# A Macaron block on one core: new order of the head, and weight preparation moved between engines and steps

## Chip, cores and metric

The kernel runs on one core of a Trainium2 chip. The metric is the time of one execution in microseconds, the median of the runs made. In the profile PE is TensorE (PEld its weight loads), DVE is VectorE, ACT is ScalarE, POOL is GpSimd, SP is SyncE, which only issues DMAs here.

## The reference

`x` has the shape (4, 512, 512). The block adds half of a routed FFN, then causal attention with 32 query heads in 8 groups (head size 128, rotary positions), then half of the same FFN again:

```python
x = x + 0.5 * ffn(layernorm(x))
x = x + attn(layernorm(x))
x = x + 0.5 * ffn(layernorm(x))
...
def ffn(h):
    query = h @ Wq.T
    router_scores = (query @ Wr.T) @ (aux_keys @ Wr.T).T / sqrt(48) + log_rel
    top_idx = top_k(router_scores, 8)
    w = softmax(query . aux_keys[top_idx] / sqrt(64) + log_rel[top_idx])
    aux_out = (w @ aux_values[top_idx]) @ Wvd.T @ Wvu.T
    log_var = log1p(var(h))
    learned = gelu(h @ Wu1.T + bu1) @ Wu2.T + bu2
    u = clip(log_var / (mean(log_var) + 1e-6) * 0.5 + sigmoid(learned) * 2.5, 0, 5)
    gate = sigmoid(gate_w1 * clip((u - 0.5) / 1.5, 0, 1) + gate_bias)
    return h + where(gate < 0.05, 0, gate) * aux_out
```

The mean of `log_var` runs over all 2048 rows, so the gate of the first row needs the variances of the whole input.

## The kernel before

**Tiles.** X stays in SBUF as 16 tiles of 128 rows. Every fp32 operand of a large matmul is split into a high part (bf16 or fp16, a cast on ACT) and a low part (the rest in fp16, a subtraction on POOL or DVE), and a product is three matmuls (`mm3`, L1522 to L1524). Attention's weights come as 256 KB pieces (K, Q0 to Q3, V and W0 to W3 for each of 8 groups). A piece is loaded into one of 8 slots of `raw` (`raw_load`, L486), its high part is a cast on ACT (`weight_high`, L801), its low part a subtraction on POOL (`weight_low`, L621) or, for the pieces in `BYDVE`, on DVE (L1201). Pieces 0 to 3 get both parts on POOL. Then the piece is kept in HBM (`keep`, L510), and batches 1 to 3 load it from there (`load_kept`, L519). `raw_load(r)` needs the low part of piece r-8, and SP issues all of this in one order.

**The head** (0 to about 69 us) is written out by hand for each engine. It does the first FFN for batch 0 and prepares the first 16 pieces. SP and ACT issue the loads. `bu2`, `gw`, `gb` (three loads of 0.5 KB, L505) are the last that count on the semaphore `ld_fs`; DVE waits for all six of that semaphore before its first `take_scores` (L1080). Then, for each of four tiles, DVE takes the scores out of PSUM and picks the top eight (`top`, L1095 to L1104), which lets ACT take the exponentials (`exps_ffn`, L781) and PE transpose them ("ET", L1592). Row sums and sums of squares of tiles 6 to 10 (`sums`, L852) are ACT's, the statistics of the others DVE's (L1022). After all variances are there (`moments_of_sums`, L1261 to L1264, `variance_logs`, L1123 to L1125) ACT takes the logarithms (`logs`, L775), DVE sums them (L1129), PE adds over the partitions ("MEAN", L1586), and the gates follow (`gs`, L1169). `aux_first` (L1271) adds the FFN to X, the second layer norm is normalised (L1059) and transposed (L1542), and the projections of group 0 begin. PE's tasks take PSUM banks in turn in the order of the list `HEAD`: a task waits until the one four places earlier is consumed. GELU needs a table load on ACT before it and another behind it (L764, L771).

**The loop** has 128 steps, one for each batch, group and head. In a step DVE takes the masked minima of the scores (`minima`, L1237), makes the low part of the step before's probabilities (`p_lo`, L1247), the reciprocal of the sums (L1389) and three products for the rotation of a later query (L1191 to L1193). POOL adds them (L629) and makes the query's low part (L634), ACT the exponentials (L831) and high parts. SP transposes the probabilities by DMA (`turn`, L526), two issues a step, behind that step's loads and keeps. In batch 0 the steps also prepare pieces 16 and on: `REFILL` says which pieces belong to which of a group's four steps; `MADE_AT` is the step in which a piece is made. It is kept two steps later, and the load of the piece eight places later follows the keep. FFN work of the next batch (`side`) is spread over the steps by tables. In step 0 DVE refines the deviation of tiles 4 to 15 (`deviation`, L1036 to L1040, `base_factors`, L1044, L1045); steps 0 and 1 normalise the first two tiles of batch 1 (L1059).

Of the kernel before, what the change touches and what calls it, by code (L numbers as in the profile page):

```python
# [12 lines left out]
P = 128  # L13
# [16 lines left out]
NSPLIT = 4  # L30
BYDVE = range(6, 11)

# [24 lines left out]
NRAW = 8  # L57
# [48 lines left out]
def rest_of(n, h):  # L106
# [4 lines left out]

HEAD = ([("LT", 0, 0, i) for i in range(4)] + [("QRY", 0, 0, 0), ("SCR", 0, 0, 0), ("SCR", 0, 0, 1), ("HID", 0, 0, 0), ("ET", 0, 0, 0),
        ("HOUT", 0, 0, 0), ("MEAN", 0, 0, 0)] + [("AUX", 0, 0, i) for i in range(4)] + [("LT", 1, 0, i) for i in range(4)])
FIRST = [("V", 0, 0, 0), ("K", 0, 0, 0), ("Q", 0, 0, 0), ("Q", 0, 1, 0)]
# [34 lines left out]
def prepared(engine, what):  # L149
    return PREPARED[engine].index(what) + 1  # L150

REFILL = {0: [(1, "Q1"), (1, "V"), (-1, "W3")], 1: [(1, "Q2")], 2: [(1, "Q3"), (2, "K"), (0, "W0")],
          3: [(2, "Q0"), (0, "W1"), (0, "W2")]}
# [23 lines left out]
for s_ in range(NS):  # L179
    for it_ in made(s_):  # L180
        ITEMS.append(it_)
        MADE_AT.append(s_)
ITEM = {it: r for r, it in enumerate(ITEMS)}
NHEAD = len(HEAD_ITEMS)


def macaron_kernel(nc: bass.Bass, x, wqkv, wo, bo, cosq, sinq, cosk, sink,
# [3 lines left out]
    with ctx:  # L191
# [289 lines left out]
        def _(sp):  # L481
# [20 lines left out]
            load_x(12, 4)  # L502
            for dst, src in ((bu2[:, :], f_bu2.to_broadcast([P, 1])), (gw[:, :], f_gw.to_broadcast([P, 1])),
                             (gb[:, :], f_gb.to_broadcast([P, 1]))):
                sp.dma_start(dst, src).then_inc(ld_fs, 16)  # L505

# [48 lines left out]
            for s in range(NS):  # L555
                for n, kind in refills(s):
                    if n >= G or (n, kind) in STAGED:
                        load_kept(n, kind)
                for r in range(NHEAD, len(ITEMS)):
                    if MADE_AT[r] + 2 == s:  # L560
                        keep(r)
                for r in range(NHEAD + NRAW, len(ITEMS)):
                    if MADE_AT[r - NRAW] + 2 == s:
                        raw_load(r)
                if s:
                    turn(s - 1, 0)
                    turn(s - 1, 1)
                for _, k, bb, i in side(SP_A, SP_B, s):
                    turn_normal(k, bb, i)
# [9 lines left out]
        def _(pool):  # L579
# [76 lines left out]
            nc.gpsimd.tensor_tensor(ul[:, :, :], fwu1T, uh[:, :, :], ALU.subtract).then_inc(fu_lo, 1)  # L656
            pool.wait_ge(x_ab[0], 1)
            for n in range(4):
                nc.gpsimd.tensor_scalar(X[:, n, :], X[:, n, :], xa[:, 0, n:n + 1], xb[:, 0, n:n + 1], ALU.mult,
                                        ALU.add).then_inc(x_up[0], 1)  # L660
            for r in range(NSPLIT):
                weight_low(r)
            pool.wait_ge(r_gs[0], 1)
            for r in range(NSPLIT, BYDVE[0]):
                weight_low(r)
            pool.wait_ge(rope_lo, 2)
            pool.wait_ge(w_lo, BYDVE[-1] + 1)
            weight_low(BYDVE[-1] + 1)
            rope("Q", 0, 1)
            for r in range(BYDVE[-1] + 2, NHEAD):  # L670
                weight_low(r)
# [31 lines left out]
        def _(act):  # L703
            roots, totals = [0], [0]
            for n in (0, 2):
                act.dma_start(X[:, n:n + 2, :], x_v[:, n:n + 2, :]).then_inc(ld_x[n], 16)
            for dst, src in ((lrb[:, :], f_lr.to_broadcast([P, NSLOT])), (bu1[:, :], f_bu1), (wu2T[:, :], f_wu2T)):
                act.dma_start(dst, src).then_inc(ld_fs, 16)
# [146 lines left out]
            def sums(n):  # L855
                act.wait_ge(ld_x[n // 4 * 4], 16)
                total(n, ACT.Identity, s1[:, 0, n:n + 1])
                total(n, ACT.Square, s2[:, 0, n:n + 1])
# [22 lines left out]
            nc.scalar.activation(bh[:, 0:NSLOT], SC[:, 1, 0:NSLOT], ACT.Copy, scale=fqs[:, 0:1]).then_inc(fs_act, 1)  # L881
            nc.scalar.activation(bh[:, NSLOT:2 * NSLOT], fkeyT[:, :], ACT.Copy, scale=fqs[:, 0:1]).then_inc(fs_act, 1)
            query_hi(0, 0, 0)
            query_hi(0, 0, 1)
            act.wait_ge(ld_fu, 16)
            nc.scalar.copy(uh[:, :, :], fwu1T).then_inc(fs_act, 1)
            for n in BYACT[:3]:
                sums(n)
            exps_ffn(0, 0, (0, 1))
            sums(BYACT[3])  # L890
            exps_ffn(0, 0, (2, 3))
            sums(BYACT[4])
            act.wait_ge(ld_fs, 96)
            gelu(0, 0)
            e_hi(0, 0)
            gate_exp(0, 0, 4)
            logs(0)
            act.wait_ge(fs_pe, prepared("pe", "v2"))
            nc.scalar.copy(v2h[:, :], PV[:, :]).then_inc(fs_act, 1)
            weight_high(4)  # L900
            gate_exp(1, 0, 4)
# [111 lines left out]
        def _(dve):  # L1013
# [305 lines left out]
            query_lo(0, 0, 1)  # L1319
            base_factors(0, 0, 4)  # L1320
            arrived(4)
            arrived(5)
            dve.wait_ge(ld_fs, 96)
            for i in range(2):
                take_scores(0, 0, (i,))
                top(0, 0, (i,))
            dve.wait_ge(ld_x[8], 16)
            moments(0, 11)
            arrived(12)
            for i in range(2, 4):  # L1330
                take_scores(0, 0, (i,))
                top(0, 0, (i,))
            for n in range(13, NT):
                moments(0, n)
            dve.wait_ge(fs_pe, prepared("pe", "u1T"))
            nc.vector.tensor_copy(u1T[:, :], SC[0:VB, 0, 0:NSLOT]).then_inc(fs_dve, 1)
            variance(0, 4, NT)
            moments_of_sums()
            dve.wait_ge(ln_v[0], 3)
            variance_logs(0)  # L1340
            learned(0, 0)
            gate_1(0, 0, 4, 1)
            e_lo(0, 0)
            sigmoid(0, slice(0, 4))
            log_sum(0)
            dve.wait_ge(fs_act, prepared("act", "v2"))
            nc.vector.tensor_tensor(v2l[:, :], PV[:, :], v2h[:, :], ALU.subtract).then_inc(fs_dve, 1)
            inverse_sums(0, 0, 4, 1)
            log_mean(0)
# [10 lines left out]
            for i in range(4):  # L1360
                turned_lo(1, 0, i)
            for r in BYDVE:
                weight_low(r)
# [11 lines left out]
            for s in range(NS):  # L1375
                n, h = divmod(s, HG)
                par = s % 2
                minima(s)
                if s == 0:
                    deviation(0, 1, 4, NT)  # L1380
                    base_factors(0, 4, NT)
                if s:
# [11 lines left out]
                for stage, k, bb, i in side(DVE_A, DVE_B, s):  # L1394
                    if stage == "nrm":
                        normal(k, bb, i)
# [121 lines left out]
        def _(pe):  # L1518
# [220 lines left out]
            ins.then_inc(fs_pe, 1)  # L1739
            ffn_task(("ET", 0, 0, 0))  # L1740
            pe.wait_ge(fs_dve, prepared("dve", "u1T"))
            mm(PV[:, :], u1T[:, :], fwvuT, start=True, stop=True).then_inc(fs_pe, 1)
            pe.wait_ge(ld_fs, 96)
            ffn_task(("HOUT", 0, 0, 0))
            ffn_task(("MEAN", 0, 0, 0))
# [84 lines left out]
```

## Time and profile before

| | us |
|---|---|
| median of three runs | 1433.54 (1432.22 to 1436.56) |
| the profiled execution | 1431.55 |
| its span | 1429.8 |
| PE busy | 1359.9 |
| DVE busy | 1184.8 |
| ACT busy | 954.0 |
| POOL busy | 701.2 |
| granted clock, mean | 0.985 |

The span is the time from the first to the last instruction; 1.75 us lie around it. Steps of the loop begin 10 to 11 us apart.

### The profile page before, as it was taken

What the parts mean: (1) busy time and instruction counts of PE and PEld (TensorE: products, weight loads), DVE (VectorE), ACT (ScalarE), POOL (GpSimd) and SP (SyncE); (2) the same over time, 40 slices, a digit from 0 to 9 for tenths busy, and PEclk for the clock granted to TensorE, in tenths of its full rate; (3) what the DMA queues carried; (4) which work ended last, traced back from release to release, by engine and by line L of the source; (5) the groups of instructions that cost most, each with busy time, mean ns of one, the idle gap of its engine ahead of it and who ended that gap; (6) DMA issues with size and microseconds to landing.
All of it is one profiled execution on the core that took longest, in us unless ns stands there. A gap on an engine that the chain in (4) does not pass through costs nothing.

```text
span 1429.8 us, 25974 instructions
## 1 busy us (share of the span) xinstructions
PE 1359.9 (95%) x8604; PEld 751.9 (53%) x8604; DVE 1184.8 (83%) x2880; ACT 954.0 (67%) x2463; POOL 701.2 (49%) x593
## 2 busy tenths in 40 slices
PE   4778999998999999999999999999999999999996
PEld 2444555454555555555555555555555555555553
DVE  6897978899988898988878798889777798778657
ACT  4567786776677677666766676667666676666754
POOL 3176666767764444345545354444544454434321
PEclk8799999999999999999999999999999999999998
DMA  8356767779677566566658656656576666556443
GB/s 302 119 138 150 191 163 186 186 173 219 171 151 163 127 144 151 118 130 148 141 124 168 130 131 146 122 134 148 138 143 127 146 142 154 116 134 135 94 88 118
DMA packets 439829, 211.21 MB, mean 148 GB/s; under 512 B 382016, under 2 KB 383344, under 8 KB 439696
## 3 DMA queue, kind: packets, MB, share of 16 engines
q1 hardware_dynamic: 438576, 208.18, 63.3%
q8 instruction: 69, 1.13, 0.3%
q10 hardware_dynamic: 1120, 1.38, 0.3%
q14 instruction: 64, 0.52, 0.1%
HBM read 91.00 MB, written 25.17 MB: 81 GB/s over the span
## 4 chain that ended last, share of the span: by engine, by line
PE 77%; DVE 12%; ACT 3%; issue 3%; POOL 2%; DMA 1%; SPq 1%; DVEq 0%; ACTq 0%
PE PJ L1522 17%; PE PJ L1524 17%; PE PJ L1523 17%; PE PV L1695 4%; PE PV L1690 4%; PE PV L1691 4%; PE SC L1709 4%; PE SC L1711 4%; PE SC L1710 4%; DVE phl L1247 3%; DVE p L1237 2%; POOL t L629 2%; DVE t L1193 1%; DVE t L1192 1%; DVE t L1191 1%
## 5 line engine op out<-in xcount | busy, mean ns | idle before, releaser
L651 POOL TENSOR_TENSOR oTl<-of,oTf 128x512 f16<-128x512 f32 x128 | 154.1, 1204 | 439.3 <-ACT oTf L823 439.0
L831 ACT ACTIVATE p<-p,mn 128x512 f32<-128x512 f32 (+3 forms) x512 | 280.9, 549 | 95.4 <-DVE mn L1237 95.4
L1247 DVE SCALAR_TENSOR_TENSOR phl<-p,ri,phl 128x128 f16<-128x128 f32 (+3 forms) x512 | 331.5, 687 | 0.0
L842 ACT ACTIVATE phl<-p,ri 128x128 f16<-128x128 f32 (+3 forms) x512 | 245.6, 550 | 4.1
L1522 PE MATMUL PJ<-XT,wsp 128*128 128x512 f16 x628 | 238.9, 380 | 4.8 <-DVE t L1193 4.8
L629 POOL TENSOR_TENSOR t<-t 128x512 f32<-128x512 f32 x158 | 201.4, 1275 | 76.4 <-DVE t L1193 75.9
L1524 PE MATMUL PJ<-XT,wsp 128*128 128x512 f16 x628 | 238.8, 380 | 0.0
L1523 PE MATMUL PJ<-XT,wsp 128*128 128x512 f16 x628 | 238.7, 380 | 0.0
L1237 DVE CUSTOM_DVE_ANT_0 p<-SC,maskw 128x512 f32<-128x512 f32 (+3 forms) x512 | 219.8, 485 | 2.2
L1522 PE MATMUL PJ<-wosp,oTf 128*128 128x512 bf16 x512 | 194.1, 379 | 0.0
L1524 PE MATMUL PJ<-wosp,oTl 128*128 128x512 bf16 x512 | 194.1, 379 | 0.0
L1523 PE MATMUL PJ<-wosp,oTf 128*128 128x512 f16 x512 | 194.1, 379 | 0.0
L634 POOL TENSOR_TENSOR qTl<-t,qTh 128x512 f16<-128x512 f32 x127 | 148.3, 1167 | 92.5 <-ACT qTh L807 92.5
L807 ACT CAST qTh<-t 128x512 bf16<-128x512 f32 x128 | 79.1, 618 | 138.2 <-POOL t L629 136.1
L1690 PE MATMUL PV<-pTf,vh 128*128 128x512 f16 (+3 forms) x512 | 146.9, 301 | 12.4 <-DMA pTf<-phl 12.4
L1709 PE MATMUL SC<-kTh,qTh 128*128 128x512 bf16 (+3 forms) x512 | 147.3, 301 | 8.4 <-DVE mn L1237 5.7
L1710 PE MATMUL SC<-kTl,qTh 128*128 128x512 f16 (+3 forms) x512 | 153.9, 301 | 0.0
L1711 PE MATMUL SC<-kTh,qTl 128*128 128x512 bf16 (+3 forms) x512 | 147.3, 301 | 0.0
L822 ACT ACTIVATE of<-PV 128x512 f32<-128x512 f32 x128 | 75.2, 587 | 96.2 <-PE PV L1695 96.2
L1691 PE MATMUL PV<-pTf,vl 128*128 128x512 f16 (+3 forms) x512 | 133.1, 301 | 0.0
L1224 DVE TENSOR_TENSOR X<-PJ,X 128x512 f32<-128x512 f32 x124 | 85.0, 686 | 35.2 <-PE PJ L1524 34.0
L1524 PEld LDWEIGHTS PJ<-XT,wsp 128*128 128x128 f16 x628 | 61.5, 98 | 74.6 <-issue 0.8
(263 smaller groups left out, 2588.7 us busy)
## 6 DMA issues: line engine op xcount, KB each, us to landing
wsp<-kept SPq DMA_DIRECT2D x146, 256.0 KB, 3.0
wosp<-kept SPq DMA_DIRECT2D x96, 256.0 KB, 3.4
raw<-in_wqkv SPq DMA_DIRECT2D x48, 256.0 KB, 4.7
kept<-wsp SPq DMA_DIRECT2D x42, 256.0 KB, 2.4
raw<-in_wo SPq DMA_DIRECT2D x32, 256.0 KB, 4.7
kept<-wosp SPq DMA_DIRECT2D x32, 256.0 KB, 3.0
pTf<-phl SPq DMA_TRANSPOSE x256, 3.8
X<-in_x SPq DMA_DIRECT2D x3, 1024.0 KB, 9.6
```

The lines of the kernel that those rows point to most:

```text
L629: ins = nc.gpsimd.tensor_tensor(t1[:, j, c], t1[:, j, c], t2[:, j, c], ALU.add)
L831: ins = nc.scalar.activation(pt, pt, ACT.Exp, bias=mn[:, par, i:i + 1], scale=-1.0, accum_out=rs[:, par, i:i + 1])
L842: nc.scalar.activation(phl[:, par, high(i, 0):high(i, i) + 1:3, :], p[:, par, SOFF[i]:SOFF[i] + w].rearrange("p (k t) -> p k t", t=P), ACT ...
L1237: ins = nc.vector.tensor_tensor_reduce(out=p[:, par, SOFF[i]:SOFF[i] + w], in0=SCf[:, SOFF[i]:SOFF[i] + w], in1=maskw[:, T - w:T], scale=1 ...
L1247: nc.vector.scalar_tensor_tensor(out=phl[:, par, low(i, 0):low(i, i) + 1, :], in0=p[:, par, SOFF[i]:SOFF[i] + w].rearrange("p (k t) -> p k ...
L1522: mm(out_, lh, rh, start=start, stop=False)
L1523: mm(out_, lh, rl, start=False, stop=False)
L1524: return mm(out_, ll, rh, start=False, stop=stop)
L1690: mm(PV[:, j * P:T], vh[:, n % 2, j, :], hi, start=j == 0, stop=False)
L1709: mm(o, qh, kh, start=True, stop=False)
L1710: mm(o, qh, kl, start=False, stop=False)
L1711: ins = mm(o, ql, kh, start=False, stop=True)
```

## The change

- The three small loads `bu2`, `gw`, `gb` are issued by ACT behind its own, and no longer by SP.
- The head is reordered. DVE selects tiles 0 and 1 before it takes the statistics of tiles 4 and 5, takes `u1T` ahead of tiles 2 and 3, and has `learned` and `gate_1` before the last five statistics. ACT copies `uh` before the queries, takes GELU before any exponentials, and puts its sums between them. PE does HOUT before the product for `v2` and before ET.
- POOL waits for the first two selections before it scales X, and for all four before it makes the low parts of pieces 0 to 3. It now makes 6, 7 and 8 too, after the second layer norm's tiles are normalised, and 12 ahead of the rotation of Q1. DVE keeps 9 and 10 only.
- The deviation of tiles 4 to 15 and the normalisation of batch 1's first two tiles leave steps 0 and 1 and stand before DVE's low parts and the rotation of K.
- A group's V piece is loaded or made in step 1 of four, not in step 0. A raw load comes one step before its piece is made (for W2 in the same step), a keep two steps after (for W2 three).

```diff
-BYDVE = range(6, 11)
+BYDVE = range(9, 11)
...
-HEAD = ([...] + [("QRY", 0, 0, 0), ("SCR", 0, 0, 0), ("SCR", 0, 0, 1), ("HID", 0, 0, 0), ("ET", 0, 0, 0),
-        ("HOUT", 0, 0, 0), ("MEAN", 0, 0, 0)] + ...
+HEAD = ([...] + [("QRY", 0, 0, 0), ("SCR", 0, 0, 0), ("SCR", 0, 0, 1), ("HID", 0, 0, 0), ("HOUT", 0, 0, 0),
+        ("ET", 0, 0, 0), ("MEAN", 0, 0, 0)] + ...
...
-REFILL = {0: [(1, "Q1"), (1, "V"), (-1, "W3")], 1: [(1, "Q2")], 2: [(1, "Q3"), (2, "K"), (0, "W0")],
+REFILL = {0: [(1, "Q1"), (-1, "W3")], 1: [(1, "Q2"), (1, "V")], 2: [(1, "Q3"), (2, "K"), (0, "W0")],
           3: [(2, "Q0"), (0, "W1"), (0, "W2")]}
...
+RAW_AT = [at - (0 if kind == "W2" else 1) for at, (n, kind) in zip(MADE_AT, ITEMS)]
+KEEP_AT = [at + (3 if kind == "W2" else 2) for at, (n, kind) in zip(MADE_AT, ITEMS)]
...
-            for dst, src in ((bu2[:, :], f_bu2.to_broadcast([P, 1])), (gw[:, :], f_gw.to_broadcast([P, 1])),
-                             (gb[:, :], f_gb.to_broadcast([P, 1]))):
-                sp.dma_start(dst, src).then_inc(ld_fs, 16)
...
-                    if MADE_AT[r] + 2 == s:
+                    if KEEP_AT[r] == s:
                         keep(r)
...
-                    if MADE_AT[r - NRAW] + 2 == s:
+                    if RAW_AT[r] == s:
                         raw_load(r)
...
             pool.wait_ge(x_ab[0], 1)
+            pool.wait_ge(r_mn[0], 2)
             for n in range(4):
                 nc.gpsimd.tensor_scalar(X[:, n, :], ...).then_inc(x_up[0], 1)
+            pool.wait_ge(r_mn[0], 4)
             for r in range(NSPLIT):
                 weight_low(r)
             pool.wait_ge(r_gs[0], 1)
-            for r in range(NSPLIT, BYDVE[0]):
+            for r in range(NSPLIT, 6):
                 weight_low(r)
-            pool.wait_ge(rope_lo, 2)
+            pool.wait_ge(ln_h[1], 4)
+            for r in range(6, BYDVE[0]):
+                weight_low(r)
             pool.wait_ge(w_lo, BYDVE[-1] + 1)
             weight_low(BYDVE[-1] + 1)
+            pool.wait_ge(rope_lo, 2)
+            weight_low(BYDVE[-1] + 2)
             rope("Q", 0, 1)
-            for r in range(BYDVE[-1] + 2, NHEAD):
+            for r in range(BYDVE[-1] + 3, NHEAD):
                 weight_low(r)
...
+            act.wait_ge(ld_fu, 16)
+            nc.scalar.copy(uh[:, :, :], fwu1T).then_inc(fs_act, 1)
             query_hi(0, 0, 0)
             query_hi(0, 0, 1)
-            act.wait_ge(ld_fu, 16)
-            nc.scalar.copy(uh[:, :, :], fwu1T).then_inc(fs_act, 1)
-            for n in BYACT[:3]:
-                sums(n)
-            exps_ffn(0, 0, (0, 1))
-            sums(BYACT[3])
-            exps_ffn(0, 0, (2, 3))
-            sums(BYACT[4])
+            sums(BYACT[0])
+            sums(BYACT[1])
             act.wait_ge(ld_fs, 96)
             gelu(0, 0)
-            e_hi(0, 0)
-            gate_exp(0, 0, 4)
-            logs(0)
+            exps_ffn(0, 0, (0, 1))
             act.wait_ge(fs_pe, prepared("pe", "v2"))
             nc.scalar.copy(v2h[:, :], PV[:, :]).then_inc(fs_act, 1)
+            sums(BYACT[2])
+            exps_ffn(0, 0, (2, 3))
+            gate_exp(0, 0, 4)
+            sums(BYACT[3])
+            e_hi(0, 0)
+            sums(BYACT[4])
+            logs(0)
...
             base_factors(0, 0, 4)
+            dve.wait_ge(ld_fs, 96)
+            select_first(0)
+            select_first(1)
             arrived(4)
             arrived(5)
-            dve.wait_ge(ld_fs, 96)
-            for i in range(2):
-                take_scores(0, 0, (i,))
-                top(0, 0, (i,))
+            dve.wait_ge(fs_pe, prepared("pe", "u1T"))
+            nc.vector.tensor_copy(u1T[:, :], SC[0:VB, 0, 0:NSLOT]).then_inc(fs_dve, 1)
+            select_first(2)
+            select_first(3)
+            learned(0, 0)
+            gate_1(0, 0, 4, 1)
             dve.wait_ge(ld_x[8], 16)
             moments(0, 11)
             arrived(12)
-            for i in range(2, 4):
-                take_scores(0, 0, (i,))
-                top(0, 0, (i,))
             for n in range(13, NT):
                 moments(0, n)
...
             variance_logs(0)
-            learned(0, 0)
-            gate_1(0, 0, 4, 1)
+            sigmoid(0, slice(0, 4))
             e_lo(0, 0)
-            sigmoid(0, slice(0, 4))
-            log_sum(0)
             dve.wait_ge(fs_act, prepared("act", "v2"))
             nc.vector.tensor_tensor(v2l[:, :], PV[:, :], v2h[:, :], ALU.subtract).then_inc(fs_dve, 1)
+            log_sum(0)
...
                 turned_lo(1, 0, i)
+            deviation(0, 1, 4, NT)
+            base_factors(0, 4, NT)
+            normal(0, 1, 0)
+            normal(0, 1, 1)
             for r in BYDVE:
                 weight_low(r)
...
-                if s == 0:
-                    deviation(0, 1, 4, NT)
-                    base_factors(0, 4, NT)
...
-            ffn_task(("ET", 0, 0, 0))
+            pe.wait_ge(ld_fs, 96)
+            ffn_task(("HOUT", 0, 0, 0))
             pe.wait_ge(fs_dve, prepared("dve", "u1T"))
             mm(PV[:, :], u1T[:, :], fwvuT, start=True, stop=True).then_inc(fs_pe, 1)
-            pe.wait_ge(ld_fs, 96)
-            ffn_task(("HOUT", 0, 0, 0))
+            ffn_task(("ET", 0, 0, 0))
```

`select_first(i)` is `take_scores` and `top` of tile i.

## Rows read from the trace of the kernel before

**Rows 1.** One stretch: length; busy PE, PEld, DVE, ACT, POOL (instructions); clock; DMA share; GB/s.

```profile
84.00:108.00 24.00, 16.38 (x128) 9.42 (x126) 22.00 (x40) 15.32 (x39) 16.06 (x13) 1.00 0.58 110
```

**Rows 2.** What TensorE waited for, 130 to 370 us: total, times, longest.

```profile
PE PV L1690 <- DMA pTf<-phl: 6.7, 3, 4.0
...
PE PJ L1522 <- DVE t L1193: 4.8, 3, 2.4
```

**Rows 3.** The same view, 370 to 1370 us.

```profile
PE PV L1695 <- DMA pTf<-phl: 0.4, 1, 0.4
```

**Rows 4.** Chain that ended last: start, length, what.

```profile
14.96 8.82 DMA gb<-in_f_gb
```

**Rows 5.** Timeline of VectorE, head: start, length, line, operation, count, idle before.

```profile
18.68 1.28 DVE L1022 BATCH_NORM_STATS2 st<-X 128x6 f32<-128x512 f32 x2
...
23.81 0.29 DVE L1080 SCALAR_TENSOR_TENSOR rsc<-PJ,lrb 128x128 f32<-128x128 f32 x1 [3.85 <-DMA gb<-in_f_gb]
...
28.98 1.28 DVE L1022 BATCH_NORM_STATS2 st<-X 128x6 f32<-128x512 f32 x2
...
30.18 0.27 DVE L1080 SCALAR_TENSOR_TENSOR rsc<-PJ,lrb 128x128 f32<-128x128 f32 x1
...
33.59 1.87 DVE L1022 BATCH_NORM_STATS2 st<-X 128x6 f32<-128x512 f32 x3
...
36.05 0.15 DVE L1261 TENSOR_SCALAR s<-s 128x5 f32<-128x5 f32 x1
...
37.20 0.17 DVE L1125 TENSOR_TENSOR gv<-mv,nv 128x16 f32<-128x16 f32 x1
...
41.36 0.17 DVE L1129 TENSOR_REDUCE lsum<-lv 128x1 f32<-128x16 f32 x1
```

**Rows 6.** DMA issues of the first 70 us: queue, count, KB, us to landing.

```profile
wu2T<-in_f_wu2T ACTq DMA_DIRECT2D x1, 0.5 KB, 7.5
```

**Rows 7.** Timeline of GpSimd, head.

```profile
19.90 3.02 POOL L659 TENSOR_SCALAR X<-X,xa,xb 128x512 f32<-128x512 f32 x4
...
22.86 0.62 POOL L616 CAST wsp<-raw 128x512 bf16<-128x512 f32 x1
...
28.99 1.15 POOL L621 TENSOR_TENSOR wsp<-raw,wsp 128x512 f16<-128x512 f32 x1
```

**Rows 8.** Timeline of ScalarE, head.

```profile
18.51 0.72 ACT L852 ACTIVATE t<-X 128x512 f32<-128x512 f32 x1
...
22.65 0.19 ACT L852 ACTIVATION_READ_ACCUMULATOR t<-X 128x1 f32 x1
...
38.01 1.28 ACT L771 ACT_TABLE_LOAD   x1
```

**Rows 9.** VectorE's small operation in step 0, and GpSimd beside it.

```profile
71.21 1.17 DVE L1039 TENSOR_SCALAR nw<-nw 128x12 f32<-128x12 f32 x1
...
72.31 2.27 POOL L621 TENSOR_TENSOR oTl<-raw,oTl 128x512 f16<-128x512 f32 x2
```

**Rows 10.** Timeline of TensorE, head.

```profile
41.68 0.55 PE L1586 MATMUL PJ<-lsum,ones 128*128 128x1 f32 x2 [1.71 <-DVE lsum L1129]
```

**Rows 11.** VectorE between the second layer norm's transposes and the rotation of K.

```profile
56.16 2.49 DVE L1201 TENSOR_TENSOR wosp<-raw,wosp 128x512 f16<-128x512 f32 x4
...
59.60 0.69 DVE L1191 TENSOR_TENSOR t<-PJ,ck 128x512 f32<-128x512 f32 x1 [0.36 <-PE PJ L1524]
```

**Rows 12.** VectorE and GpSimd in steps 0 to 2.

```profile
76.79 1.59 DVE L1059 TENSOR_SCALAR hb<-X,mv,rstd 128x512 f32<-128x512 f32 x1
...
76.84 1.26 POOL L629 TENSOR_TENSOR t<-t 128x512 f32<-128x512 f32 x1
...
94.36 0.18 DVE L1389 RECIPROCAL ri<-rs 128x4 f32<-128x4 f32 x1 [1.80 <-ACT p L831]
```

**Rows 13.** SyncE's queue in a step of the second batch.

```profile
714.21 0.32 SPq L519 DMA_DIRECT2D wosp<-kept  x1
...
717.44 3.97 SPq L526 DMA_TRANSPOSE pTf<-phl  x2
```

More of the change, by code:

```diff
@@ L109, in rest_of @@
     return [t for t in r if 0 <= t[1] < NU]
-HEAD = ([("LT", 0, 0, i) for i in range(4)] + [("QRY", 0, 0, 0), ("SCR", 0, 0, 0), ("SCR", 0, 0, 1), ("HID", 0, 0, 0), ("ET", 0, 0, 0),
-        ("HOUT", 0, 0, 0), ("MEAN", 0, 0, 0)] + [("AUX", 0, 0, i) for i in range(4)] + [("LT", 1, 0, i) for i in range(4)])
+HEAD = ([("LT", 0, 0, i) for i in range(4)] + [("QRY", 0, 0, 0), ("SCR", 0, 0, 0), ("SCR", 0, 0, 1), ("HID", 0, 0, 0), ("HOUT", 0, 0, 0),
+        ("ET", 0, 0, 0), ("MEAN", 0, 0, 0)] + [("AUX", 0, 0, i) for i in range(4)] + [("LT", 1, 0, i) for i in range(4)])
 FIRST = [("V", 0, 0, 0), ("K", 0, 0, 0), ("Q", 0, 0, 0), ("Q", 0, 1, 0)]
@@ L706, in _ @@
                 act.dma_start(X[:, n:n + 2, :], x_v[:, n:n + 2, :]).then_inc(ld_x[n], 16)
-            for dst, src in ((lrb[:, :], f_lr.to_broadcast([P, NSLOT])), (bu1[:, :], f_bu1), (wu2T[:, :], f_wu2T)):
+            for dst, src in ((lrb[:, :], f_lr.to_broadcast([P, NSLOT])), (bu1[:, :], f_bu1), (wu2T[:, :], f_wu2T),
+                             (bu2[:, :], f_bu2.to_broadcast([P, 1])), (gw[:, :], f_gw.to_broadcast([P, 1])),
+                             (gb[:, :], f_gb.to_broadcast([P, 1]))):
                 act.dma_start(dst, src).then_inc(ld_fs, 16)
@@ L1320, in _, with select_first @@
             base_factors(0, 0, 4)
+            dve.wait_ge(ld_fs, 96)
+            def select_first(i):
+                take_scores(0, 0, (i,))
+                top(0, 0, (i,))
+            select_first(0)
+            select_first(1)
             arrived(4)
             arrived(5)
-            dve.wait_ge(ld_fs, 96)
-            for i in range(2):
-                take_scores(0, 0, (i,))
-                top(0, 0, (i,))
+            dve.wait_ge(fs_pe, prepared("pe", "u1T"))
[4 more added lines that the diff above has]
+            gate_1(0, 0, 4, 1)
             dve.wait_ge(ld_x[8], 16)
@@ L1329, in _ @@
             arrived(12)
-            for i in range(2, 4):
-                take_scores(0, 0, (i,))
-                top(0, 0, (i,))
             for n in range(13, NT):
                 moments(0, n)
-            dve.wait_ge(fs_pe, prepared("pe", "u1T"))
-            nc.vector.tensor_copy(u1T[:, :], SC[0:VB, 0, 0:NSLOT]).then_inc(fs_dve, 1)
             variance(0, 4, NT)
@@ L1394, in _ @@
                 for stage, k, bb, i in side(DVE_A, DVE_B, s):
-                    if stage == "nrm":
+                    if stage == "nrm" and (k, bb, i) not in ((0, 1, 0), (0, 1, 1)):
                         normal(k, bb, i)
```

## The prediction

> **What bounds the kernel now.** I read three views in this order: PE's waits by stretch, the chain that ended last, and the timelines of the head. From 370 to 1370 us PE waited for 0.4 us in all [rows 3]: there it is the bound, its work is unchanged, and nothing done to other engines can save time. Time can be won only where PE stands idle: in the head, in the first steps of the loop (PE busy 16.4 of 24 us against VectorE's 22.0, [rows 1]), and in single waits of batch 0 [rows 2]. What PE saves there moves the whole rest forward.
>
> In the head the chain lies for 8.82 us on the load of `gb` [rows 4]. SP issued it at 14.96 us behind a dozen others, and VectorE, done with two statistics at 19.9, stood idle for 3.85 us until 23.81 [rows 5]. From there VectorE's four selections, ScalarE's exponentials and sums, the variances, the logarithms and the mean follow in one chain up to MEAN at 41.68 [rows 10]. Behind MEAN the change leaves the order as it is up to the transposes of the second layer norm. So I work out when MEAN starts, then what changes behind it.
>
> **Part 1, the gates' loads.** They are now issues four to six of ScalarE's own group, some 0.45 us each, so out by about 4.6 us. The load in front of them took 7.5 us to land [rows 6]; the slowest of the three took 8.8 in its old place [rows 4]. They land by 13.5 us at the worst, 5 us before they are needed. ScalarE's table load slips by 1.4 us, covered by its wait for the first variances. So the selections start at about 18.7 instead of 23.8.
>
> **Part 2, up to the mean.** Two tiles without GpSimd beside them took 30.18 to 33.59, 1.7 us each; with it 23.81 to 28.98, 2.6 each [rows 5]. The new waits keep GpSimd away from tiles 0 and 1: done at 22.1. Two statistics (1.2 us at their pitch) and `u1T` (0.2) bring 23.6, two more tiles 27.0. GpSimd's four scalings of X, 3.02 us [rows 7], now lie beside tile 2; I add 0.5 (bounds 0 and 1.8, what four tiles' neighbours cost before): 27.6. `learned`, `gate_1`, five statistics at 0.6 and seven aggregates (0.5) end at 31.6 on VectorE. ScalarE's way is longer: each `sums` costs 1.42 us (three of them, six operations with their reads, lay from 18.51 to 22.84), a table load 1.28 [rows 8]. Two sums end at 21.0, the loads and GELU at 24.3, then two exponentials, v2 and one sums (27.5); exponentials 2 and 3 end at 28.6, and two sums, `e_hi` and a gate operation bring 32.3. The chain of variances then runs on VectorE: 36.05 to 37.37, 1.32 us for seven operations [rows 5]. Alone that gives 33.6.
>
> But GpSimd now begins pieces 0 to 3 behind the last selection, at about 27.9. They took 22.86 to 30.14, 7.3 us [rows 7], so it works until 35.2, on top of this chain. Before, it stood idle there. How such small operations fare is seen in step 0: 12 columns took 1.17 us where they take 0.17 alone, ending with GpSimd's operation in progress [rows 9]; the reciprocal beside it was not held. So until 35.2 one VectorE operation passes per GpSimd operation, about three of the seven, and four more cost 0.8: 36.0. The bounds are 33.6 (none held) and 36.0 plus 1.0 (each of the first four meets a long one). I take 36.0, nearest to those rows. By the seven operations' own rows, 0.15 to 0.25 us each, it would be 33.6 and the head 2.4 us shorter. The Trainium skill (GPSIMD Engine Reference, Key points) lists contention "with DVE instructions in a 2-port perf mode or with two SBUF inputs"; five or six of the seven are of these kinds, so by that rule they are held, and it speaks against the place chosen for pieces 0 to 3.
>
> Behind it come two operations of the sigmoid, `e_lo` and `v2l`, 1.6 us, now ahead of the sum of the logarithms: 37.6, MEAN at 37.9 in place of 41.68 [rows 10]. **Term: -3.8** (bounds -6.1 and -2.8).
>
> **Part 3, before the loop.** Of five low parts on VectorE, 2.49 us for four [rows 11], two stay (1.24). Added are four linked operations (0.8), the base factors (0.2) and two normalisations (0.5 each when alone): 3.3 in place of 3.1, and there were 0.36 us idle before the rotation of K [rows 11]. That alone is even. GpSimd, idle there before, now makes piece 8 beside the linked operations: one is held by about a microsecond. The rotation of K and the whole chain to the first scores on VectorE slip. **Term: +0.9** (bounds 0 and +3, every added operation held once).
>
> **Part 4, steps 0 to 2.** VectorE loses 3.7 us of the deviation and its factors (held to over 1 us each, [rows 9]) and two normalisations of 1.59 [rows 12]. Step 0's minima must wait for ScalarE's exponentials anyway, so of this 2.7 us reach step 1, and 1.6 more step 2. But the query's path runs over GpSimd, whose addition began at 76.84 right behind its low parts [rows 12]; one part fewer there lets it start 1.0 us earlier. In step 2 VectorE had to wait 1.80 us for exponentials [rows 12], which hang on that path. So what arrives at step 3 is about 2 us. **Term: -2.0** (bounds 0 and -4.3).
>
> **Part 5, pieces in batch 0.** Per four steps it was 3, 1, 3, 3 pieces with 6, 2, 6, 6 keeps and loads; now 2, 2, 3, 3 with five in each step. PE's waits that this can touch are 6.7 us for transposed probabilities, the longest 4.0 behind a step with seven transfers, and 4.8 us for rotations [rows 2]. The raw loads come later, but still a step ahead of the cast. The 4.0 should shrink by the two transfers fewer, the rest moves at random. **Term: -1.5** (bounds -5 and +2). In batches 1 to 3 V's load moves too; PE waits there for nothing [rows 3]: 0.
>
> **Sum:** -3.8 + 0.9 - 2.0 - 1.5 = -6.4. The profiled execution took 1431.55 us (span 1429.8 and 1.75 around it), which gives 1425.2. The median of the three runs lies 2.0 above it, so I forecast 1427.
>
> **Rivals.**
> *Not held (better).* The variance chain passes GpSimd, or the sums end earlier: -6.1; nothing held before the loop: 0; steps 0 to 2: -4; batch 0: -3. In all -13, 1420.5. For it: the bounds of each term. Against: [rows 9]. Chance 0.2.
> *The head gains, the loop gives nothing.* Steps 0 to 2 are set by GpSimd and ScalarE, not by VectorE, and batch 0's waits only change places: -3.8 + 0.9 = -2.9, 1430.6. For it: VectorE's 1.80 us of waiting in step 2 with ScalarE as its releaser. Against: VectorE's 22.0 of 24 us busy. Chance 0.22.
> *Slower: V's load before the probabilities.* In step 1 of each group SP issues two loads instead of one ahead of the transposes. If these are already late, each of the 24 groups of batches 1 to 3 loses the issue, about 0.5 us: +12, net +6, 1439. It decides from the point where less than 0.5 us lies between the loads and the transposes. Against: the last load of such a step was out at 714.5 and the transposes began at 717.44 [rows 13], and steps with three loads cost PE nothing [rows 3]. Chance 0.05.
> *The change does nothing.* Had `gb` not been the true last, selections would still start at 23.8. But X, scores and bias were there before 19.9. Chance 0.03.
>
> **Numbers.** The forecast case has 0.5, with a range of its own from 1423.5 to 1430. What a measurement here can tell from no change is 0.3%, 4.3 us: faster is below 1429.2. That takes in the better rival and most of the forecast's case, 0.72; within 0.3% the second rival, the fourth and the forecast's rest, 0.23; slower 0.05. The range 1418 to 1431.5 reaches into the two neighbouring rivals.
>
> **What the profile after should show.** No wait of VectorE for `gb`, selections from 18.7. MEAN at 37 to 38; if it is near 35.5, nothing was held. Operations of L1261 to L1125 with a microsecond each if I am right. K's rotation 52 to 57 us (before 59.60). The fourth step's scores some 5 us earlier than before. PE's waits between 130 and 370 us at 10 to 14 us. I am wrong if `sums` (L852) end well after 32.3, or if waits for `pTf` turn up after 420 us.

## The result and the profile after

| | median, us | runs | ratio to before | 95% interval |
|---|---|---|---|---|
| before | 1434.25 | 4 | | |
| after | 1426.04 | 4 | 0.9945 | 0.9926 to 0.9964 |

The change is faster by 0.55% (0.36% to 0.74%), about 8 us. The forecast was 1427 with 1418 to 1431.5. The profiled execution took 1426.41 us, its span 1423.6, 6.2 less than before. Measured again beside other kernels, the same kernel gave 0.9942 (0.993 to 0.9955).

Between the two traces the span fell by 6.2 us and the whole time by 5.1, while the medians fell by 8.2. The profiled execution of before (1431.55) was 2.7 us faster than its median, that of after 0.4 slower than its own. Only one trace of before exists, and no trace shows where its slower executions lose their time.

Where the 6.2 us of the traces came from can be read by lining them up at the same work (a shift is after minus before; a step begins with VectorE's first minima):

| where | before, us | after, us | shift |
|---|---|---|---|
| first selection starts | 23.81 | 18.93 | -4.88 |
| MEAN starts | 41.68 | 37.03 | -4.65 |
| second layer norm's transposes | 51.50 | 46.53 | -4.97 |
| rotation of K starts | 59.60 | 55.66 | -3.94 |
| step 0, VectorE's first minima | 69.16 | 65.22 | -3.94 |
| step 1 | 78.31 | 71.60 | -6.71 |
| step 2 | 89.58 | 82.38 | -7.20 |
| step 3 | 98.91 | 93.08 | -5.83 |
| step 34 | 428.22 | 422.77 | -5.45 |

The timeline of VectorE after (columns as in [rows 5]) shows the selections without a wait for `gb`, and then the variance chain, whose first and last operation before stand in [rows 5]:

```profile
18.93 0.28 DVE L1089 SCALAR_TENSOR_TENSOR rsc<-PJ,lrb 128x128 f32<-128x128 f32 x1
...
20.64 0.29 DVE L1089 SCALAR_TENSOR_TENSOR rsc<-SC,lrb 128x128 f32<-128x128 f32 x1
...
23.75 0.27 DVE L1089 SCALAR_TENSOR_TENSOR rsc<-PJ,lrb 128x128 f32<-128x128 f32 x1
...
25.98 0.29 DVE L1089 SCALAR_TENSOR_TENSOR rsc<-SC,lrb 128x128 f32<-128x128 f32 x1
...
32.12 0.17 DVE L1270 TENSOR_SCALAR s<-s 128x5 f32<-128x5 f32 x1
32.32 1.00 DVE L1271 TENSOR_TENSOR mv<-X,s 128x5 f32<-128x5 f32 x1
...
33.42 0.46 DVE L1273 SCALAR_TENSOR_TENSOR mv<-s,dm 128x5 f32<-128x5 f32 x1
...
34.13 0.25 DVE L1133 RECIPROCAL nv<-nv 128x16 f32<-128x16 f32 x1
34.42 0.72 DVE L1134 TENSOR_TENSOR gv<-mv,nv 128x16 f32<-128x16 f32 x1
...
36.72 0.16 DVE L1138 TENSOR_REDUCE lsum<-lv 128x1 f32<-128x16 f32 x1
```

Two operations of the same chain in before:

```profile
36.23 0.17 DVE L1262 TENSOR_TENSOR mv<-X,s 128x5 f32<-128x5 f32 x1
...
36.91 0.25 DVE L1124 RECIPROCAL nv<-nv 128x16 f32<-128x16 f32 x1
```

The second operation took 1.00 us where it took 0.17 before, the last 0.72, also for 0.17; the reciprocal between took 0.25 as before. GpSimd beside them (after, timeline; before it is [rows 7]):

```profile
22.64 3.01 POOL L660 TENSOR_SCALAR X<-X,xa,xb 128x512 f32<-128x512 f32 x4 [4.91 <-DVE mnr L1113]
27.84 0.61 POOL L616 CAST wsp<-raw 128x512 bf16<-128x512 f32 x1 [2.19 <-DVE mnr L1113]
...
32.11 1.18 POOL L621 TENSOR_TENSOR wsp<-raw,wsp 128x512 f16<-128x512 f32 x1
33.24 0.62 POOL L616 CAST wsp<-raw 128x512 bf16<-128x512 f32 x1
33.95 1.16 POOL L621 TENSOR_TENSOR wsp<-raw,wsp 128x512 f16<-128x512 f32 x1
...
51.39 1.16 POOL L621 TENSOR_TENSOR wosp<-raw,wosp 128x512 f16<-128x512 f32 x1 [1.28 <-ACT wosp L809]
```

VectorE's held operations ended at 33.32, 33.88 and 35.14; GpSimd's operations in progress ended at 33.29, 33.86 and 35.11. The last row is piece 8. It holds the first of the added operations on VectorE in front of the rotation of K (1.14 us). These are VectorE's rows in the place of [rows 11]:

```profile
51.43 1.14 DVE L1045 TENSOR_TENSOR nw<-rstd 128x12 f32<-128x12 f32 x1
52.61 0.17 DVE L1046 SCALAR_TENSOR_TENSOR nw<-mv,nw 128x12 f32<-128x12 f32 x1
...
53.39 1.00 DVE L1068 TENSOR_SCALAR hb<-X,mv,rstd 128x512 f32<-128x512 f32 x2
...
55.66 0.69 DVE L1200 TENSOR_TENSOR t<-PJ,ck 128x512 f32<-128x512 f32 x1
```

What PE waited for, 60 to 125 us, then 125 to 370 us ([rows 2] begin at 130), then 370 to 1370 us [rows 3], three views of after:

```profile
PE PV L1703 <- DMA pTf<-phl: 4.1, 2, 2.6
PE SC L1722 <- POOL qTl L634: 2.8, 2, 1.4
PE SC L1722 <- DVE mn L1246: 2.6, 1, 2.6
```

```profile
PE PJ L1535 <- DVE t L1202: 3.9, 3, 2.1
PE PV L1703 <- DMA pTf<-phl: 2.6, 1, 2.6
PE PV L1708 <- DMA pTf<-phl: 2.0, 1, 2.0
```

```profile
PE PV L1703 <- DMA pTf<-phl: 1.1, 1, 1.1
PE PV L1708 <- DMA pTf<-phl: 1.1, 2, 0.8
```

Each row gives the total, the number of times and the longest, in us. From 370 us on nearly all is at the end of batch 0 (at 372.75 and 374.83 us); behind that PE is all but free of waits, as before. Between steps 3 and 28 all of PE's listed waits came to 19.7 us before and 16.5 after. PE's busy time there rose from 252.3 to 255.1 us and the stretch took 0.4 us longer, so the shorter waits bought no time. What lengthened the busy time is not shown.

### The profile page after: what moved, and what is told of

Read it like the earlier page. It is cut to its first block, busy times and chain, and to the rows that moved or that the text cites. A ratio compares the mean times of both kernels' runs of the same rounds, so it can differ in the third digit from the quotient of the medians.

```text
span 1423.6 us, 25847 instructions
## 1 busy us (share of the span) xinstructions
PE 1351.8 (95%) x8474; PEld 754.3 (53%) x8604; DVE 1177.8 (83%) x2877; ACT 953.3 (67%) x2463; POOL 704.9 (50%) x596
## 4 chain that ended last, share of the span: by engine, by line
PE 70%; DVE 15%; ACT 5%; issue 4%; POOL 4%; DMA 1%; DVEq 0%; SPq 0%; ACTq 0%
PE PJ L1536 16%; PE PJ L1537 15%; PE PJ L1535 15%; DVE phl L1256 4%; PE PV L1708 4%; PE PV L1703 4%; PE PV L1704 4%; PE SC L1724 4%; PE SC L1722 4%; PE SC L1723 4%; POOL t L629 2%; ACT p L839 2%; DVE p L1246 2%; DVE t L1202 2%; DVE t L1200 1%
## 5 line engine op out<-in xcount | busy, mean ns | idle before, releaser
L1537 PE MATMUL PJ<-wosp,oTl 128*128 128x512 bf16 x475 | 180.0, 379 | 0.0
L1535 PE MATMUL PJ<-wosp,oTf 128*128 128x512 bf16 x432 | 163.7, 379 | 1.9
```

Of the source, the lines that this page charges most:

```text
L1535: mm(out_, lh, rh, start=start, stop=False)
L1537: return mm(out_, ll, rh, start=False, stop=stop)
```

## Experiments

Twelve further measurements were made, one of them of the unchanged kernel after, each with the kernel before in the same rounds. The medians of before differ between these groups (1434.6, 1432.66, 1433.84), so the ratios are compared. "b" is the kernel before with one part of the change; "a" is the kernel after with one thing taken back or added.

| kernel | edit | median | ratio to before | interval |
|---|---|---|---|---|
| b_loads | only the gates' loads | 1430.15 | 0.9973 | 0.9964 to 0.9982 |
| a_loads | without them | 1431.83 | 0.9985 | 0.9976 to 0.9994 |
| b_refill | only the spread of pieces | 1432.66 | 0.9987 | 0.9979 to 0.9996 |
| a_refill | without it | 1426.44 | 0.9954 | 0.9941 to 0.9966 |
| a_loopdev | deviation back in the loop | 1426.60 | 0.9947 | 0.9928 to 0.9967 |
| a_nowait | GpSimd without its waits | 1426.12 | 0.9948 | 0.9933 to 0.9963 |
| a_logsum | logarithms' sum first | 1425.14 | 0.9943 | 0.9925 to 0.996 |
| a_pool | pieces 0 and 1 in idle times | 1424.86 | 0.9942 | 0.9926 to 0.9958 |
| after_again | none | 1425.53 | 0.9942 | 0.993 to 0.9955 |
| a_order | K first on GpSimd in step 1 | 1421.74 | 0.9915 | 0.99 to 0.993 |
| a_plo | low part ahead of a wait | 1423.01 | 0.9926 | 0.9912 to 0.9939 |
| a_all | a_logsum, a_pool, a_order and a_plo together | 1419.76 | 0.9902 | 0.9888 to 0.9915 |

**The loads alone (b_loads).**

```diff
-            for dst, src in ((bu2[:, :], ...), (gw[:, :], ...), (gb[:, :], ...)):
-                sp.dma_start(dst, src).then_inc(ld_fs, 16)
...
-            for dst, src in ((lrb[:, :], ...), (bu1[:, :], f_bu1), (wu2T[:, :], f_wu2T)):
+            for dst, src in ((lrb[:, :], ...), (bu1[:, :], f_bu1), (wu2T[:, :], f_wu2T), (bu2[:, :], ...), (gw[:, :], ...), (gb[:, :], ...)):
                 act.dma_start(dst, src).then_inc(ld_fs, 16)
```

> The kernel before, with only the three gates' loads moved from SP to ScalarE's queue. My theory (the wait is real, but the selections are then held by GpSimd's work beside them and ScalarE's late GELU stays in the path): selections start at 19.9 us instead of 23.8, MEAN starts 2 to 3 us earlier than 41.68, whole time 2 to 3 us shorter than before. Rival, the chain's share taken at its word: 4 us or more shorter. Rival, another chain hides the wait: within 1 us of before.

Selections start at 19.56, MEAN at 38.44, 3.24 us earlier than before. Of this 2.1 are left at the rotation of K, which here waits 1.49 us for PE (first its timeline of VectorE; then two stretches of b_loads, and two of before, with columns as in [rows 1], the clock third from the end):

```profile
57.50 0.69 DVE L1190 TENSOR_TENSOR t<-PJ,ck 128x512 f32<-128x512 f32 x1 [1.49 <-PE PJ L1523]
```

```profile
52.00:54.00 2.00, 2.00 (x23) 2.00 (x21) 1.84 (x4) 2.00 (x5) 0.00 (x0) 0.54 0.00 0
54.00:56.00 2.00, 2.00 (x21) 1.29 (x19) 2.00 (x4) 1.39 (x3) 0.00 (x0) 1.00 0.69 194
```

```profile
52.00:54.00 2.00, 2.00 (x11) 2.00 (x10) 1.42 (x3) 1.10 (x2) 0.00 (x0) 0.50 0.00 0
54.00:56.00 2.00, 2.00 (x30) 1.99 (x29) 1.74 (x3) 1.73 (x5) 0.00 (x0) 0.89 0.00 0
```

In b_loads PE had been idle for 4.01 us before its work resumed at 48.01. Its granted clock was 0.50 (1.2 GHz) from 48 to 52 us, 0.54 from 52 to 54 and 1.00 (2.4 GHz) behind it, so the transposes and part of the projections of K ran at the lower level. Before had the same 4.01 us of idle time, up to 51.50, but its clock was back at 0.89 in the stretch from 54 to 56. So b_loads ran some 3 us longer at the lower level (an estimate from these stretches), and the rotation's wait for PE, 1.49 us where it was 0.36 [rows 11], is where 1.1 of the 3.24 us went.

The ratio says 3.9 us (2.6 to 5.2): more than my 2 to 3, and the rival of 4 us or more is inside its interval. The trace cannot add to this, as it is of the slowest of the ten executions: still 2.1 us early at step 3, it was 0.9 late by step 34. The traces show only this much: of the chain's 8.82 us [rows 4], 3.24 came out at MEAN.

**The change without the loads (a_loads).** The reverse of the edit above, on the kernel after.

> The kernel after, with the three loads back on SP. My theory (all of the new order hangs on the early selections): selections start at about 23.8 us instead of 18.9, MEAN near 42 instead of 37.0, whole time 4 to 5.5 us longer than after, so 1430 to 1431.5. Rival (the reordered sums of ScalarE set the end of the chain, and have slack to give): 2 us or less longer than after.

Selections at 24.38, MEAN at 43.13: later even than before's 41.68. Of the difference 0.57 us is the wait for `gb` itself, which ended later here; from the first selection to MEAN it took 18.75 us, against 17.87 before. The whole lies 5.7 us over after by the ratios (0.9985 against 0.9945). So the new order in the head is worth nothing by itself, it is made for early selections; the two belong together. Step 0 was 1.86 us later than before, step 3 level with it: the change in steps 0 to 2 (part 4) brought these 1.9 us.

**The spread of pieces (a_refill, b_refill).**

```diff
-REFILL = {0: [(1, "Q1"), (-1, "W3")], 1: [(1, "Q2"), (1, "V")],
+REFILL = {0: [(1, "Q1"), (1, "V"), (-1, "W3")], 1: [(1, "Q2")],
...
-                    if KEEP_AT[r] == s:
+                    if MADE_AT[r] + 2 == s:
...
-                    if RAW_AT[r] == s:
+                    if MADE_AT[r - NRAW] + 2 == s:
```

> The kernel after, with the old spread of pieces over the steps of a group and the old times of raw loads and keeps. By my forecast's term (-1.5 us for the spread) it is 1.5 us longer than after. Rival (waits in batch 0 only change places; the two traces differ by +0.4 us between step 3 and step 34): within 1 us of after, and the shift against before is the same at step 3 and at step 34 to 1 us.

> The kernel before with the new spread of pieces and the new times of raw loads and keeps alone. By my forecast's term 1.5 us shorter than before. Rival (only moves waits): within 1 us of before. Second rival (V's load ahead of the transposes costs): longer than before, with waits for the transposed probabilities after 370 us.

In the trace of a_refill the shift against before is -5.97 at step 3, -5.98 at step 33 and -5.02 at step 34. After itself has -5.83, -5.46 and -5.45, with detours to -8.25 between. b_refill goes from +0.60 to +0.82 and +0.84. By these three the spread brings nothing. But the traces cannot settle it: all thirteen other traces, with either spread, took 0.2 to 3.0 us longer than before's from step 4 to step 34 (with the old spread a_refill 0.95, b_loads 3.0), so the one trace of before is a fast one there.

The timed runs speak for the spread: b_refill is 1.9 us under before (0.6 to 3.0, which leaves out 0), a_refill some 1.3 us over after with intervals that overlap. And a_loads, which has the spread and is level with before at step 3, is 2.2 us under it by its ratio. So the forecast 1.5 us stands within what was timed, and no trace shows where it lies.

What the spread does to single waits of PE is alike in the five traces compared (after, after_again, b_refill with it, before and a_refill without). The wait for the probabilities near 328 us (334 in before and b_refill) is 2.6 to 2.7 us with it, 1.3 and 1.4 without. The wait for a rotation near 262 us (268) is 1.3 to 1.5 us with it, 2.4 without. The second rival fell: PE's waits from 370 us on were 2.0 us in b_refill and 0.6 in a_refill, far from 12.

**The deviation (a_loopdev).** `deviation(0, 1, 4, NT)`, `base_factors` and the two `normal` calls move back into steps 0 and 1.

> The kernel after, with the deviation of tiles 4 to 15 and the normalisation of batch 1's first two tiles back in steps 0 and 1. My theory (parts 3 and 4, net -1.1 us): the rotation of K starts 0.7 us earlier than after (55.66), but step 3's minima 1 to 1.5 us later than after's 93.08, and the whole is 1 to 1.5 us longer than after. Rival (steps 0 to 2 are set by GpSimd and ScalarE): step 3 as after or earlier, no loss.

Rotation of K at 55.19, step 0 at -4.41, steps 1 to 3 at -5.48 against before: only 0.35 us behind after at step 3, where I had expected 1 to 1.5. The whole (0.9947 against 0.9945) shows no loss either. The deviation in step 0 lies mostly in VectorE's wait for the exponentials (2.46 us there in after). The step from -4.41 to -5.48 came without moving it, from GpSimd, which has one low part fewer between the rotations: its additions start 6.56 us apart there, 7.63 before. And without the added operations in front of it the rotation of K is still not free, it waits for PE:

```profile
55.19 0.69 DVE L1200 TENSOR_TENSOR t<-PJ,ck 128x512 f32<-128x512 f32 x1 [1.40 <-PE PJ L1536]
```

**GpSimd's waits (a_nowait).** The two `pool.wait_ge(r_mn[0], ...)` are taken out; nothing else needs them.

> The kernel after without GpSimd's two waits for the selections (it scales X and makes pieces 0 to 3 as soon as it can). My theory (GpSimd holds VectorE's operations beside it, wherever it lies): the four selections take about 2.5 us longer in all, the variance chain from L1270 to L1134 takes 1.3 us instead of 2.9, MEAN starts 0.5 to 1.5 us later than 37.03, whole 0.5 to 1.5 us longer than after. Rival (the waits are needless): MEAN 1.6 us earlier.

First to fourth selection start 9.33 us apart (18.67 to 28.00), against 7.05 in after; the variance chain took 1.35 us against 3.02. From the first selection to MEAN 18.69 us against 18.10. So GpSimd's work costs much the same in the other place, 0.6 us more; the whole is level with after (0.9948 against 0.9945).

**Pieces in idle times (a_pool).**

```diff
+            weight_low(0)
             pool.wait_ge(x_ab[0], 1)
             pool.wait_ge(r_mn[0], 2)
...
+            weight_low(1)
             pool.wait_ge(r_mn[0], 4)
-            for r in range(NSPLIT):
-                weight_low(r)
+            weight_low(2)
+            weight_low(3)
```

(and VectorE's `base_factors(0, 0, 4)` behind the second selection)

> The kernel after, with GpSimd's piece 0 in its idle time before the first selection's compare, piece 1 between X's scaling and the end of the fourth selection, and only pieces 2 and 3 behind it (the factors of X stand behind the second selection). My theory (the variance chain is held only because GpSimd works beside it): the seven operations from L1270 to L1134 take 1.3 us instead of 2.9, MEAN starts at about 35.5 us instead of 37.03, whole 1.3 to 1.6 us shorter than after. Rival (small operations are slow there for another reason): the seven take 2.9 us whatever GpSimd does.

Timeline of VectorE in a_pool; the first, second and last of the seven operations L1270 to L1134 of after:

```profile
33.05 0.17 DVE L1272 TENSOR_SCALAR s<-s 128x5 f32<-128x5 f32 x1
33.26 0.17 DVE L1273 TENSOR_TENSOR mv<-X,s 128x5 f32<-128x5 f32 x1
...
34.23 0.17 DVE L1136 TENSOR_TENSOR gv<-mv,nv 128x16 f32<-128x16 f32 x1
```

1.35 us for the seven, the same instructions with the same operands. Holding is GpSimd's doing. But 0.7 us of it came back in front, in the selections beside pieces 0 and 1 and in the factors moved between them: first selection to MEAN 17.17 us, 0.93 less than after; step 0 at -4.98 instead of -3.94. The timed whole does not show it: 0.9942, the same as after_again, where I had expected 1.3 to 1.6 us. The intervals, some 4.5 us wide, are too wide to tell one microsecond.

**The sum of the logarithms (a_logsum).** `log_sum(0)` stands ahead of `e_lo` and `v2l`. In after it stood behind both, in the kernel before between them.

> The kernel after, with the sum of the logarithms ahead of e_lo and v2l on VectorE instead of behind them. My theory (in after the two, 1.3 us, lie in the path of MEAN): MEAN starts at about 36.0 instead of 37.03, gs at 39.3 instead of 40.14, whole 0.8 to 0.9 us shorter than after. Rival (the logarithms or the auxiliary products end last): nothing.

First selection to MEAN 16.88 us, 1.22 less than after. Less than half of that reaches the loop. Counted from the first selection (0.36 us late in this execution), the first operation on MEAN's result is only 0.69 us earlier (at 37.37), as `e_lo` and `v2l` now stand in front of it on VectorE. At the rotation of K, which waits 0.27 us for PE, 0.48 are left, at step 0 0.47. The whole, 0.9943, shows nothing of the 0.8 to 0.9 us expected.

**What step 3 gives back (a_order, a_plo).** Step 2 was 7.2 us early, step 3 only 5.8. The timelines of after name the reason: VectorE waits 2.06 us for ScalarE's exponentials, these stand behind the cast of K in ScalarE's queue, and that waits 3.14 us for GpSimd, which does a low part of the layer norm (`hl`) first:

```profile
88.72 0.18 DVE L1402 RECIPROCAL ri<-rs 128x4 f32<-128x4 f32 x1 [2.06 <-ACT p L839]
```

```profile
85.88 0.62 ACT L815 CAST kTh<-t 128x512 bf16<-128x512 f32 x1 [3.14 <-POOL t L629]
86.40 0.72 ACT L839 ACTIVATE p<-p,mn 128x512 f32<-128x512 f32 x1
```

```profile
82.30 1.16 POOL L634 TENSOR_TENSOR qTl<-t,qTh 128x512 f16<-128x512 f32 x1 [0.73 <-ACT qTh L815]
83.41 1.16 POOL L608 TENSOR_TENSOR hl<-hb,hl 128x512 f16<-128x512 f32 x1
84.53 1.32 POOL L629 TENSOR_TENSOR t<-t 128x512 f32<-128x512 f32 x1
```

```diff
+                if s == 1:
+                    rope("K", 1, 0)
                 for stage, k, bb, i in side(POOL_A, POOL_B, s):
```

> The kernel after, unchanged, as the measure of the three beside it. MEAN near 37.0, step 3's minima near 93.1, median 1425.5 to 1427, or 7.5 to 9 us under the kernel before. It tells how far the head's times move by themselves.

> The kernel after, with GpSimd's addition for the rotation of K ahead of its low part of the layer norm in step 1. My theory (what step 1 gave in the change is lost again in step 2, because ScalarE's exponentials stand behind the cast of K, and that hangs on GpSimd's queue): the cast of K starts 1.1 us earlier than 85.88, step 3's minima about 1 us earlier than 93.08, whole 0.5 to 1 us shorter than after. Rival (the transposed probabilities are what PE waits for): step 3's minima earlier, but no shorter whole.

The cast of K in a_order (timeline of ScalarE):

```profile
83.96 0.62 ACT L817 CAST kTh<-t 128x512 bf16<-128x512 f32 x1 [1.98 <-POOL t L629]
```

It waits 1.98 us instead of 3.14. Steps 0 to 2 are 0.76 us earlier than after (the head's own scatter), step 3 is 2.90 and step 4 3.63 earlier, and it stays. So the swap brought 2.1 us by step 3 and 2.9 by step 4, more than the 1.16 us of the one operation. VectorE's operations behind the swap were held less: the first three low parts of the probabilities (L1247 of before) took 1.73 and 2.18 us in steps 2 and 3 against 2.63 and 4.14 in after, the normalisation in step 2 0.55 against 1.59. That this makes up the rest is my reading; no run takes it apart. By the ratios it is 3.9 us under after_again, and the intervals just touch. I had expected 0.5 to 1.

In a_plo the fourth `p_lo` of steps 1 and 2 stands ahead of the wait for the exponentials:

```diff
                     p_lo(s - 1, 2)
+                if s in (1, 2):
+                    p_lo(s - 1, 3)
                 dve.wait_ge(a_exp, 3 * s + 3)
```

> The kernel after, with VectorE's fourth low part of the probabilities ahead of its wait for the exponentials in steps 1 and 2. My theory (it stands needlessly behind a wait of 0.96 and 2.06 us, and the transposes behind it): the transposes of step 1's probabilities are issued 1.5 to 2 us earlier, PE's wait of 2.58 us for them shrinks to about 1, step 3's minima 1 to 1.5 us earlier, whole 1 us shorter than after. Rival (VectorE's reciprocal is only later by the same amount): nothing.

The head of this execution was late (step 0 at +1.35 against after), step 2 at +0.19, step 3 at -0.44: 1.8 us won between. PE's wait for the transposes stayed, 2.65 us at 90.75. By the ratios it is 0.9926 against 0.9942 for after_again, 2.3 us with intervals that overlap. The traces show step 3 earlier without a shorter wait for the transposes, so half of the theory fell.

**Together (a_all).**

> The kernel after with all four edits together: GpSimd's pieces 0 to 3 in its idle times, the sum of the logarithms first, the rotation of K first on GpSimd in step 1, and the fourth low part of the probabilities ahead of the wait in steps 1 and 2. If the savings add: MEAN at about 35.0, step 3's minima at 89 to 90 instead of 93.08, whole 3 to 4 us shorter than after, 1422.5. Rival (PE or the transposes take over as the bound in steps 1 to 3): 2 us shorter or less.

1419.76 us, 0.9902: 5.8 us under after_again in the same rounds, with intervals that do not overlap, and 14 under before. First selection to MEAN took 15.57 us, 2.53 less than after (MEAN at 35.83, not 35.0, as the first selection came at 20.26). Step 3 at 88.93. The four edits by themselves came to 3.9, 2.3, 0 and 0 us by the ratios (a_order, a_plo, a_pool, a_logsum), which adds up within the intervals; I had expected 3 to 4. This is the fastest of the kernels tried.

## Why the prediction was right, point by point

The sum was -6.4 and the trace shows -6.2 of span. The medians moved by 8.2, so the forecast of 1427 was 1 us too high. Term by term:

| term | forecast | in the trace | |
|---|---|---|---|
| parts 1 and 2, to MEAN | -3.8 | -4.65 | within its bounds |
| part 3, to the rotation of K | +0.9 | +0.71 | |
| part 4, steps 0 to 2 | -2.0 | -1.89 | step 0 to step 3 |
| part 5, batch 0 | -1.5 | +0.38 | step 3 to step 34 |
| rest | 0 | -0.75 | step 34 to the end |

*Part 2.* The order of events was as forecast: 18.9, 27.7 for the end of the selections (forecast 27.6), 32.1 for the variances (32.3). The held chain cost 3.02 us in place of 1.32, where I had counted 3.7; that is most of the 0.9 us by which the term was too small. Three operations of seven were held, as supposed, but by 0.83, 0.29 and 0.55 us: each for what was left of one of GpSimd's operations. a_pool and a_nowait show that it is GpSimd. Without the holding MEAN would have been at about 35.4 (37.03 less the 1.67 us between 3.02 and a_pool's 1.35). The Trainium skill's rule (GPSIMD Engine Reference, Key points) fits the chain's rows: the three operations held have two SBUF inputs; the reciprocal and the statistics, with one, ran beside GpSimd at their own 0.25 and 0.6 us. But in after two TENSOR_SCALAR operations with one SBUF input were held too, at 24.97 (0.76 us for 0.23) and at 27.95 (0.53 for 0.17), as was the one of [rows 9]. The rule's other half names a 2-port perf mode; no view here shows in which mode an operation ran.

*Part 3.* The size was right, +0.71 for +0.9, and one operation was held by a microsecond, as forecast. But the reason was not the whole: in a_loopdev, which has none of the added operations in that place, MEAN to the rotation of K still takes 18.31 us, against 18.63 in after and 17.92 before. So the added work accounts for 0.3 of the 0.7 us. In a_loopdev the rest is a wait of 1.40 us for PE, where before had 0.36. PE's granted clock stood at 0.50 (1.2 GHz) there from 46 to 50 us and at 0.80 in the next 2. The forecast took PE's work as ready in time; that the term came out right is in part luck.

*Part 4.* The size was right, the reason only in part. Between steps 0 and 3 after gained 1.89 us on before and a_loopdev 1.07, the latter without moving the deviation; what moving it adds there is paid for by 0.47 in front of step 0, so it is worth 0.35 net. What I had named as the limit, the exponentials' dependence on GpSimd's queue, is shown by a_order: it hid more than 2 us.

*Part 5* is the part whose reason fell: "The 4.0 should shrink by the two transfers fewer". That wait, shortly before step 28, is 2.0 us in after, but in a_refill, with the old spread, it is 2.55 as well, so most of its shrinking is not the spread's. Another wait grew by 1.3 us with the new spread and one shrank by 1. In size the traces show nothing of the 1.5 us (+0.38 in after), while the timed runs show 1.9 (0.6 to 3.0) for b_refill; this stays open. That the sum of the traces came out at -6.2 in spite of the +0.38 is owed to the head, 0.9 us better than its term, and to the 0.75 behind step 34, which is inside what two executions differ by. So the closeness of -6.4 and -6.2 is partly luck: errors of 0.9, 0.2, 0.1, 1.9 and 0.75 us cancelled.

*Part 1* had one thing unseen, the last section tells it. The rivals: "not held" was refuted by the chain's rows, "the loop gives nothing" by steps 0 to 3, V's load by PE's waits of 2.2 us in all from 370 us on (0.4 before) where it had named 12. "The change does nothing" was refuted by the selections at 18.93.

## What to carry to other kernels

A wait that heads a chain is worth what its next rival leaves: 8.8 us on the chain bought 3 at MEAN alone, and more only with the order behind it changed too. Short linked operations on VectorE are worth placing where GpSimd is idle: beside it three of seven were held here, for 1.7 us in all. But follow such a saving to the loop before you count it: of 1.2 us at MEAN in a_logsum 0.5 reached step 0. When a saving fades within a few steps, follow the first wait behind it through the queues it passes: here one operation in front of another on GpSimd (a_order, 3.9 us by the ratios) was worth more than moving VectorE's work out of steps 0 and 1 (a_loopdev, nothing measurable). And do not price a part of 1 or 2 us from one trace on each side: traces of near-equal loops differed by up to 3 us over 30 steps.

## What the runs showed that was not expected

The forecast took 0.45 us for the issue of a DMA. The last of the three loads now in ScalarE's queue took from 0.50 to 2.75 us to issue, and ScalarE's table load stands behind it. Timelines of ScalarE, first after, then a_all:

```profile
4.17 0.65 ACTq L716 DMA_DIRECT2D gb<-in_f_gb  x1
4.85 1.28 ACT L873 ACT_TABLE_LOAD   x1 [4.85 <-issue]
7.72 0.30 ACT L724 ACTIVATE lvar<-mv,eps 128x4 f32<-128x4 f32 x1 [1.59 <-DVE mv L1037]
```

```profile
4.86 2.75 ACTq L720 DMA_DIRECT2D gb<-in_f_gb  x1
7.63 1.28 ACT L877 ACT_TABLE_LOAD   x1 [7.63 <-issue]
8.93 0.30 ACT L728 ACTIVATE lvar<-mv,eps 128x4 f32<-128x4 f32 x1
```

In after the table load ended 1.6 us before it was needed. In a_all it did not, and the first layer norm began 1.2 us late; a_plo lost 0.9 in the same way. The forecast had called this slip covered "by its wait for the first variances", at 1.4 us. In SP's queue of before two loads of the FFN's weights (`wvd` and `wvu`) took 2.19 and 3.43 us to issue too; why is not shown. With the table load ahead of the three loads it could no longer slip behind them; that was not tried.
